# A hybrid block kernel on one core: dependent DVE, ACT and POOL instructions divided into steps of their own

## The chip, the cores and the metric

The kernel runs on one core of one Trainium2 chip. A core has five engines with an in-order queue each: PE (matrix products), DVE (vector work), ACT (activations), POOL (general work) and SP (which here issues DMAs). They meet through semaphores only. The metric is device time in microseconds (us) of one launch; lower is better.

## What is computed

Sixteen sequences of 512 tokens and 256 channels, float32, go through four residual layers:

```python
x = x + mamba(layernorm(x))        # h = exp(dt*A)*h + inp, y = <h, C> + Dp*u, 16 states, a scan over 512 tokens
x = x + ffn(layernorm(x))          # all operands of the three products rounded to FP4 in blocks of 16
x = x + linear_attention(layernorm(x))   # 16 heads of 16, features elu(.)+1, running sums over the tokens
x = x + ffn(layernorm(x))          # the same weights as above

def fp4_quant_dequant(x):          # per block of 16
    scale = max(max(abs(xb)) / 6.0, 1e-12)
    return grid(abs(xb / scale)) * sign(xb) * scale
dt = softplus(dt_low @ w_dt + b_dt) * 0.099 + 0.001
y  = (q @ kv) / (q @ ksum + 1e-6)  # per head, in linear_attention
```

## The kernel before

**Parts.** A batch (one sequence) is worked in parts. `P` is the front of the Mamba layer: load, layernorm, the products x_in, B and dt, and the softplus of dt. `M` has 32 halves of state (16 states by 2 halves of the channels); for each, ACT makes the decay (an Exp and a Square, `decay`), DVE scans over 512 tokens (`scan`, line 1187) and multiplies by C (`read_state`, L1197), and PE sums pairs of states into the bank `acc_y` (`sum_states`, L864, part `G`). `S` and `Y` finish y. `R1` takes the four tiles of 128 tokens through the first FFN (f1) and then linear attention; `R2` takes them through the second FFN (f2), whose layernorm statistics R1 has already taken.

**The FFN in instructions.** Layernorm on DVE (`stats`: a bn_stats, L1139, and a bn_aggr, L1142) with the power on POOL and the normalisation on ACT; block scales on DVE (a maximum L1082, a scaling L1084, a reciprocal L1086, of which each reads the one before); the product with the reciprocal on POOL (L527); the absolute value on ACT; the rounding on DVE (`round_mag`, L1055 and L1057, through the buffer `rounding`); the product with the scale on POOL; turns on PE copied out by ACT (`copy_out`, L667); gate and up products on PE (L896, L899), tanh on ACT (L703), gating on DVE (L1237, L1241, L1245, L1248); the same scales and rounding for the 704 hidden values; the down product (L916) and the residual on DVE (`residual`, L1215).

**Attention.** PE makes q, k and v; ACT makes exp(qk/2) (L724) and squares it (L727, into `a_exp`), copies v (L729, into `vv`); DVE makes the features `fqk` of it (L1264); ACT spreads q over even and odd heads (L734, `q_par`); scores, masked scores (POOL), numerator (PE L974, L981), the sum of k by v (`kv_new`, L1289, and `kv`, L1291), its turn (L996), the division (L1269, L1271, L1273), the turn of y (`yT`) and the projection.

**What sets the order.** The steps of all parts are interleaved by a table written by hand, `TIMES`: for each engine the beat at which a step of a part stands, counted from the part's own first beat (`PARTS_AT`; a batch is 32 beats, one for each half of state). `order_of` sorts all steps of an engine by beat, then batch, then tile. So the scan of half m stands at its beat, and a step of R1 or R2 goes between two scans as a whole, with all its instructions. `Banks` hands out the five rotating PSUM banks in PE's order; `wait_filled` and `wait_drained` are waits on them.

**Waits inside a step.** Where an instruction reads what the one before it on the same engine has written, the engine waits in between on a semaphore that the first one raises. `Chain` counts such steps (`step` and `after`). Some steps also end with a wait on their own last instruction: `round_mag` (on its signal), `residual` and both halves of the gating (on the bank drained), `dt0` and `dt1`, and the sum of kv. An example is L1053 to L1058:

```python
def round_mag(chain, val, mag, signal, b, t):
    chain.step(nc.vector.scalar_tensor_tensor(val[1], mag, ROUNDER, val[0], ALU.max, ALU.subtract))
    chain.after(dve)
    nc.vector.scalar_tensor_tensor(val[0], mag, ROUNDER, val[1], ALU.max, ALU.subtract).then_inc(signal, 1)
    dve.wait_ge(signal, upto(b, TILES, t))
```

The softplus of dt is a step of two parts on ACT (`exp0` and `log0`: Abs, Relu, Exp, three Squares; Ln, Exp, three Squares) and one on DVE (`dt0`: L1160, L1163, L1170), and again for the second half of the channels.

## Time and profile before

| what | value |
|---|---|
| median of 3 runs | 3002.25 us |
| lowest, highest | 3001.89, 3004.42 us |
| span of the profiled execution | 2998.5 us |
| PE busy | 2452.0 us (82%) |
| DVE busy | 2362.8 us (79%) |
| ACT busy | 1899.2 us (63%) |
| POOL busy | 961.6 us (32%) |

The median is 3.75 us over the span of the profiled execution; that much lies around it. A line of the profile names the engine, the line of the code, the operation and the tiles (out<-in, buffer numbers left out); in a timeline it begins with the start and the duration in us, and ends, where the engine had been idle before, with the idle time and what released it, in brackets. xN are N instructions in a row taken together.

### The profile page before, as it was taken

Reading aid. Unit: us, or ns where it says so; the run is one execution under the profiler, and the core shown is the slowest. Engines: PE = TensorE matmul, PEld = TensorE weight load, DVE = VectorE, ACT = ScalarE, POOL = GpSimd, SP = SyncE. Lnnn points to the kernel's source line nnn. Section 1 sums busy time; section 2 is a strip of 40 time slices with the busy share of each in tenths; the row PEclk is TensorE's granted clock in tenths of the full one; section 3 lists DMA queues with packets and bytes.
Section 4 is the critical chain, followed back from the end, with each engine's and each line's share of the span. In section 5 each row is a group of like instructions: output and inputs, shape, how many; then the busy total and the mean of one; then the engine's idle time right before and its main releaser. Section 6 shows DMA issues by size and latency. Waiting matters only on the chain.

```text
span 2998.5 us, 40701 instructions
## 1 busy us (share of the span) xinstructions
PE 2452.0 (82%) x12908; PEld 1394.9 (47%) x12908; DVE 2362.8 (79%) x4136; ACT 1899.2 (63%) x3677; POOL 961.6 (32%) x1632
## 2 busy tenths in 40 slices
PE   3559798888979888797978879798887979879796
PEld 1125354453535445353554535455353545536464
DVE  7776877969788796978879697887969788787744
ACT  4757567685766758576575757658575675846342
POOL 3022332333333233333323233233323323333432
PEclk7669899999999999999999999999999999989898
DMA  3431212112121221212112121211212121121000
GB/s 74 112 88 43 74 46 74 48 50 69 40 78 46 64 55 52 69 41 78 46 46 73 41 77 36 79 46 45 81 39 75 38 81 46 54 58 33 4 5 9
DMA packets 104434, 165.97 MB, mean 55 GB/s; under 512 B 15442, under 2 KB 34078, under 8 KB 104222
## 3 DMA queue, kind: packets, MB, share of 16 engines
q1 hardware_dynamic: 104222, 163.37, 19.8%
q8 instruction: 106, 1.74, 0.2%
q14 instruction: 106, 0.87, 0.1%
HBM read 146.55 MB, written 16.78 MB: 54 GB/s over the span
## 4 chain that ended last, share of the span: by engine, by line
PE 40%; DVE 35%; ACT 17%; issue 5%; POOL 2%; DMA 0%; SPq 0%; DVEq 0%; ACTq 0%; POOLq 0%
PE bank L916 10%; PE bank L899 10%; DVE scan_bufs L1187 7%; DVE scan_bufs L1197 4%; PE acc_y L864 4%; PE bank L956 3%; DVE f_h_max L1082 2%; DVE rounding L1055 2%; ACT p_xT L615 2%; ACT masked_scores L667 2%; PE bank L896 2%; PE bank L937 2%; DVE f_h L1057 2%; PE bank L909 1%; ACT scan_bufs L605 1%
## 5 line engine op out<-in xcount | busy, mean ns | idle before, releaser
L1187 DVE TENSOR_TENSOR_SCAN scan_bufs<-scan_bufs,inp_bank 128x512 f32<-128x512 f32 x512 | 617.2, 1205 | 23.4 <-ACT scan_bufs L607 12.0
L899 PE MATMUL bank<-w_gu,f_xqT 128*128 128x512 f32 x1024 | 496.0, 629 | 52.0 <-ACT f_xqT L667 23.6
L916 PE MATMUL bank<-w_dn,f_hqT 128*128 128x256 f32 (+1 forms) x1536 | 425.6, 423 | 36.3 <-ACT yT L667 33.6
L864 PE MATMUL acc_y<-scan_bufs,sel_y 128*32 128x512 f32 x1024 | 301.5, 673 | 126.9 <-DVE scan_bufs L1197 126.7
L916 PEld LDWEIGHTS bank<-w_dn,f_hqT 128*128 128x128 f32 (+1 forms) x1536 | 296.7, 207 | 155.4 <-issue 78.4
L605 ACT ACTIVATE scan_bufs<-scan_bufs,a_rows 128x512 f32<-128x512 f32 x512 | 365.4, 714 | 4.5 <-DMA scan_bufs<-dt_copy 3.8
L1197 DVE TENSOR_TENSOR scan_bufs<-scan_bufs,c_bank 128x512 f32<-128x512 f32 x512 | 343.5, 671 | 11.8 <-issue 0.2
L899 PEld LDWEIGHTS bank<-w_gu,f_xqT 128*128 128x128 f32 x1024 | 197.4, 201 | 310.1 <-issue 264.0
L607 ACT ACTIVATE scan_bufs<-scan_bufs 128x512 f32<-128x512 f32 x512 | 322.6, 630 | 16.2
L527 POOL TENSOR_TENSOR f_h<-f_h,f_h_inv 128x704 f32<-128x704 f32 x128 | 177.9, 1390 | 368.2 <-DVE f_h_inv L1086 368.2
L527 POOL TENSOR_TENSOR f_h<-f_h,f_h_scale 128x704 f32<-128x704 f32 x128 | 178.1, 1391 | 278.5 <-DVE f_h L1057 278.5
L545 POOL TENSOR_SCALAR_AFFINE_SELECT masked_scores<-masked_scores 128x512 f32<-128x512 f32 x256 | 156.4, 635 | 313.3 <-ACT masked_scores L667 313.2
L703 ACT ACTIVATE f_tanh<-bank 128x512 f32<-128x512 f32 (+1 forms) x256 | 117.3, 458 | 174.1 <-PE bank L899 159.9
L1215 DVE TENSOR_TENSOR x<-bank,x 128x256 f32<-128x256 f32 x192 | 79.9, 416 | 170.2 <-PE bank L916 161.0
L896 PE MATMUL bank<-w_gu,f_xqT 128*128 128x384 f32 x512 | 200.4, 515 | 0.2 <-DVE f_h L1237 0.2
L667 ACT ACTIVATE masked_scores<-bank 128x512 f32<-128x512 f32 x256 | 138.1, 592 | 71.1 <-PE bank L956 70.9
L956 PE MATMUL bank<-q_par,fqk 32*128 32x128 f32 x2048 | 149.0, 283 | 23.7 <-ACT f_hqT L667 8.8
L956 PEld LDWEIGHTS bank<-q_par,fqk 32*128 32x128 f32 x2048 | 125.6, 187 | 87.9 <-issue 58.8
L527 POOL TENSOR_TENSOR f_x<-f_x,f_x_scale 128x256 f32<-128x256 f32 x128 | 80.1, 626 | 259.5 <-DVE f_x L1057 259.5
L864 PEld LDWEIGHTS acc_y<-scan_bufs,sel_y 128*32 128x32 f32 x1024 | 38.5, 112 | 267.7 <-DVE scan_bufs L1197 188.5
L691 ACT ACTIVATE f_h_abs<-f_h 128x704 bf16<-128x704 f32 x128 | 101.2, 790 | 96.8 <-POOL f_h L527 96.8
L672 ACT ACTIVATE f_x<-x,f_below,f_rstd 128x256 f32<-128x256 f32 x128 | 75.8, 592 | 136.2 <-POOL f_below L520 136.2
(194 smaller groups left out, 4610.9 us busy)
## 6 DMA issues: line engine op xcount, KB each, us to landing
scan_bufs<-dt_copy SPq DMA_DIRECT2D x512, 256.0 KB, 3.7
xp<-L_attn_a_x SPq DMA_DIRECT2D x16, 512.0 KB, 4.1
dt_copy<-dt SPq DMA_DIRECT2D x32, 256.0 KB, 2.0
out<-x SPq DMA_DIRECT2D x64, 128.0 KB, 1.7
w_attn<-L_attn_b_W_attn SPq DMA_DIRECT2D x1, 768.0 KB
scan_bufs<-L_ffn_w_gate SPq DMA_DIRECT2D x1, 704.0 KB
scan_bufs<-L_ffn_w_up SPq DMA_DIRECT2D x1, 704.0 KB
masked_scores<-L_ffn_w_down SPq DMA_DIRECT2D x1, 704.0 KB
```

The lines of the kernel that those rows point to most:

```text
L527: pool.tensor_tensor(d, s, spread(scale, width), ALU.mult).then_inc(signal, 1)
L545: pool.affine_select(out=sm[r][:, 4 * g:4 * g + 4, :], in_=sm[r][:, 4 * g:4 * g + 4, :], compare_op=ALU.is_ge, fill=0.0, base=0, pattern=[ ...
L605: nc.scalar.activation(half, half, ACT.Exp, scale=a_rows[:, c, at:at + 1]).then_inc(root_ready, 1)
L607: nc.scalar.activation(half, half, ACT.Square).then_inc(bar_ready, 1)
L667: nc.scalar.activation(dst, src[:, 0:width], ACT.Copy).then_inc(done, 1)
L864: last = nc.tensor.matmul(acc_y[32 * j:32 * j + 32, :], sel_y[:, q, :], bar[slot][:, h, :], start=(q == 0), stop=(q == 3), tile_position=( ...
L896: last = nc.tensor.matmul(to[:, 0:2 * (hi - lo)], f.xqT[:, k, :], w_gu[:, k, :, lo:hi], start=(k == 0), stop=(k == DH - 1))
L899: last = nc.tensor.matmul(to[:, :], f.xqT[:, k, :], w_gu[:, k, g, lo:hi], start=(k == 0), stop=(k == DH - 1))
L916: last = nc.tensor.matmul(to[:, 0:D], f.hqT[0:n, k, :], w_dn[0:n, k, :], start=(k == 0), stop=(k == FK - 1))
L956: last = nc.tensor.matmul(to[:, at:at + P], fqk[r][rows, 1, grp, :], q_par[r][rows, odd, grp, :], start=True, stop=True)
L1187: nc.vector.tensor_tensor_scan(half, half, inp[:, :], 0.0, ALU.mult, ALU.add)\
L1197: nc.vector.tensor_tensor(half, half, c_rep[:, :], ALU.mult).then_inc(read_out, 1)
```

## The change

The steps of two or more dependent instructions are divided: each instruction (or each group without a dependence inside) becomes a step with an entry in `TIMES` and a semaphore of its own. The new steps stand 0.02 to 0.03 beats behind each other, from the beat of the undivided step on. `order_of` sorts by beat and then by batch and tile, so steps of other parts that stand within those hundredths, or at the very beat, go between. The waits at the end of steps go, since whoever reads waits for the new semaphores; so do the semaphore instruction `x4_ready` behind each R2 residual and 16 small copies behind the first kv sums. Buffers change with it: `fqk` is written and squared in place of `a_exp`, `x2` goes (R1 writes `x3`), each FFN has `x_lean` and `h_lean` in place of `rounding`, and the softplus has its buffers once for each half of the channels. ACT and PE get further waits that protect single buffers; the wait for a stored tile (`x4_stored`) moves from the projection's residual to that of the down product.

PE, POOL and SP issue the same instructions in the same order. DVE issues 16 instructions fewer (the copies), ACT as many as before; waits for an instruction that stands directly ahead on the same engine are far fewer on DVE and some fewer on ACT.

The diff, cut to the table, the helpers and the places that the prediction speaks of:

```diff
 TIMES, "act":
-        ("P", "exp0"): 21.8, ("P", "log0"): 22.6, ("P", "exp1"): 24.9, ("P", "log1"): 25.2, ("M", "decay"): -1.2,
-        ("R1", "a_qkv"): 15.0, ("R1", "a_q"): 15.1,
+        ("M", "decay"): -1.2, ("M", "square"): -1.15,
+        ("R1", "a_root"): 15, ("R1", "a_qkv"): 15.05, ("R1", "a_v"): 15.1, ("R1", "a_q"): 15.1,
+        ("P", "abs0"): 21.8, ("P", "exp0"): 21.82, ("P", "sq00"): 21.84, ...
 TIMES, "dve":
-        ("P", "dt0"): 23.1, ("P", "dt1"): 26.05,
-        ("R1", "round_h"): 9.2, ("R1", "a_proj"): 21.1, ("R2", "norm"): 0.8, ...
+        ("P", "soft0"): 23.1, ("P", "sum0"): 23.2, ("P", "dt0"): 23.3, ("P", "soft1"): 26.05, ("P", "sum1"): 26.15, ("P", "dt1"): 26.25,
+        ("R1", "lean_h"): 9.2, ("R1", "round_h"): 9.23, ("R1", "a_proj"): 21.1, ("R1", "stats2"): 21.13, ("R1", "aggr2"): 21.16,
+        ("R2", "max_x"): 0.8, ("R2", "scale_x"): 0.83, ("R2", "norm"): 0.86, ("R2", "lean_h"): 9.4, ("R2", "round_h"): 9.43, ...
...
-            def round_mag(chain, val, mag, signal, b, t):
-
-                chain.step(nc.vector.scalar_tensor_tensor(val[1], mag, ROUNDER, val[0], ALU.max, ALU.subtract))
-                chain.after(dve)
-                nc.vector.scalar_tensor_tensor(val[0], mag, ROUNDER, val[1], ALU.max, ALU.subtract).then_inc(signal, 1)
-                dve.wait_ge(signal, upto(b, TILES, t))
+            def lean(mag, val, out, signal):
+
+                nc.vector.scalar_tensor_tensor(out, mag, ROUNDER, val, ALU.max, ALU.subtract).then_inc(signal, 1)
+
+            def rounded(mag, leaned, val, ready, signal, b, t):
+
+                dve.wait_ge(ready, upto(b, TILES, t))
+                nc.vector.scalar_tensor_tensor(val, mag, ROUNDER, leaned, ALU.max, ALU.subtract).then_inc(signal, 1)
...
+            def block_max(val, width, mx, signal):
+
+                nc.vector.tensor_reduce(mx, blocks(val, width)[0], AX.X, ALU.max, apply_absolute_value=True)\
+                    .then_inc(signal, 1)
+
+            def block_scale(mx, scale, least, ready, signal, b, t):
+
+                dve.wait_ge(ready, upto(b, TILES, t))
+                nc.vector.tensor_scalar(scale, mx, TIES_DOWN / 6.0, least, ALU.mult, ALU.max).then_inc(signal, 1)
+
+            def block_inv(scale, inv, ready, signal, b, t):
+
+                dve.wait_ge(ready, upto(b, TILES, t))
+                nc.vector.reciprocal(inv, scale).then_inc(signal, 1)
...
-            def stats(norm, b, t, x):
-
-                ch.step(nc.vector.bn_stats(norm.st[t][:, :], x))
-                ch.after(dve)
+            def stats(norm, t, x):
+
+                nc.vector.bn_stats(norm.st[t][:, :], x).then_inc(norm.st_ready, 1)
+
+            def aggr(norm, b, t):
+
+                dve.wait_ge(norm.st_ready, upto(b, TILES, t))
                 dve.sem_inc(aggr_allowed, 1)
                 nc.vector.bn_aggr(norm.mv[t][:, :], norm.st[t][:, :]).then_inc(norm.mv_ready, 1)
...
                 src, done = wait_filled(dve, f.part, b, t, use)
                 nc.vector.tensor_tensor(out, src[:, 0:D], x, ALU.add).then_inc(done, 1)
-                wait_drained(dve, f.part, b, t, use)
...
                     dve.wait_ge(a_exp_ready, upto(b, TILES, t))
                     j = uses.bank_of("R1", b, t, "qk")
-                    nc.vector.scalar_tensor_tensor(fqk[r][:, :, :, :].rearrange("p a g n -> p (a g n)"), a_exp[:, :],
-                                                   1.0, banks[j][:, :], ALU.min, ALU.max).then_inc(drained[j], 1)
+                    nc.vector.scalar_tensor_tensor(flat(fqk[r]), flat(fqk[r]), 1.0, banks[j][:, :], ALU.min, ALU.max)\
+                        .then_inc(drained[j], 1)
...
                 act.wait_ge(dt_spread[slot][h], 16 * (nth + 1))
                 (c, at), half = rows_of(m), bar[slot][:, h, :]
                 nc.scalar.activation(half, half, ACT.Exp, scale=a_rows[:, c, at:at + 1]).then_inc(root_ready, 1)
+
+            def square(b, m):
+
+                n, h = divmod(m, DH)
+                half = bar[slot_of(b, n)[0]][:, h, :]
                 act.wait_ge(root_ready, upto(b, HALVES, m))
                 nc.scalar.activation(half, half, ACT.Square).then_inc(bar_ready, 1)
```

Three places where the order itself changes, all on DVE and once or more in each batch. The first is where the second half of dt (`dt1`, beat 26.05) meets the residual and statistics of R1's projection and the features of the next tile (`fqk`). Before:

```order
L1160 SCALAR_TENSOR_TENSOR p_xT<-p_xT 128x512
L1163 SCALAR_TENSOR_TENSOR sp_log<-p_xT,sp_log 128x512
L1170 SCALAR_TENSOR_TENSOR dt<-sp_log,sp_pos 128x512
L1215 TENSOR_TENSOR x_0<-bank,x 128x256
L1139 BN_STATS f_st<-x_0 128x6
L1142 BN_AGGR f_mv<-f_st 128x2
L1264 SCALAR_TENSOR_TENSOR fqk<-a_exp,bank 128x512
L1289 TENSOR_TENSOR kv_new<-bank,headmask 128x272
L1291 TENSOR_TENSOR kv<-kv,kv_new 128x16x17
L1187 SCALAR_TENSOR_TENSOR scan_bufs<-scan_bufs,inp_bank 128x512
```

and after:

```order
L1216 SCALAR_TENSOR_TENSOR p_xn<-p_xn 128x512
L1273 TENSOR_TENSOR x_0<-bank,x_0 128x256
L1335 SCALAR_TENSOR_TENSOR fqk<-fqk,bank 128x512
L1189 BN_STATS f_st<-x_0 128x6
L1222 SCALAR_TENSOR_TENSOR dt<-p_xn,dt 128x512
L1195 BN_AGGR f_mv<-f_st 128x2
L1229 SCALAR_TENSOR_TENSOR dt<-dt,sp_pos 128x512
L1359 TENSOR_TENSOR kv_new<-bank,headmask 128x272
L1364 TENSOR_TENSOR kv<-kv,kv_new 128x16x17
L1245 SCALAR_TENSOR_TENSOR scan_bufs<-scan_bufs,inp_bank 128x512
```

The three dt instructions (L1160, L1163, L1170; after, L1216, L1222, L1229) no longer stand together: the residual, fqk and the statistics go between, and the last two of them stand behind fqk.

The second place is at beat 23.1, where the rounding of h in R2 meets the same steps of another tile and the first half of dt. Before:

```order
L1055 SCALAR_TENSOR_TENSOR rounding<-f_h_abs,f_h 128x704
L1057 SCALAR_TENSOR_TENSOR f_h<-f_h_abs,rounding 128x704
L1215 TENSOR_TENSOR x_0<-bank,x 128x256
L1139 BN_STATS f_st<-x_0 128x6
L1142 BN_AGGR f_mv<-f_st 128x2
L1264 SCALAR_TENSOR_TENSOR fqk<-a_exp,bank 128x512
L1160 SCALAR_TENSOR_TENSOR p_xT<-p_xT 128x512
L1163 SCALAR_TENSOR_TENSOR sp_log<-p_xT,sp_log 128x512
L1170 SCALAR_TENSOR_TENSOR dt<-sp_log,sp_pos 128x512
L1289 TENSOR_TENSOR kv_new<-bank,headmask 128x272
```

and after:

```order
L1097 SCALAR_TENSOR_TENSOR f_h_lean<-f_h_abs,f_h 128x704
L1273 TENSOR_TENSOR x_0<-bank,x_0 128x256
L1335 SCALAR_TENSOR_TENSOR fqk<-fqk,bank 128x512
L1216 SCALAR_TENSOR_TENSOR p_xT<-p_xT 128x512
L1102 SCALAR_TENSOR_TENSOR f_h<-f_h_abs,f_h_lean 128x704
L1189 BN_STATS f_st<-x_0 128x6
L1195 BN_AGGR f_mv<-f_st 128x2
L1222 SCALAR_TENSOR_TENSOR dt<-p_xT,dt 128x512
L1359 TENSOR_TENSOR kv_new<-bank,headmask 128x272
L1229 SCALAR_TENSOR_TENSOR dt<-dt,sp_pos 128x512
```

The second instruction of the rounding (L1057; after, L1102) stood directly behind the first and ahead of the residual; it now stands behind the residual, fqk and the first dt instruction.

The third place is in R2, where the scales of the hidden values of one tile meet those of the next tile's x. Before:

```order
L1084 TENSOR_SCALAR f_h_scale<-f_h_max 128x44
L1086 RECIPROCAL f_h_inv<-f_h_scale 128x44
L1082 TENSOR_REDUCE f_x_max<-f_x 128x16
L1084 TENSOR_SCALAR f_x_scale<-f_x_max 128x16
L1086 RECIPROCAL f_x_inv<-f_x_scale 128x16
L1197 TENSOR_TENSOR scan_bufs<-scan_bufs,c_bank 128x512
```

and after:

```order
L1135 TENSOR_SCALAR f_h_scale<-f_h_max 128x44
L1129 TENSOR_REDUCE f_x_max<-f_x 128x16
L1140 RECIPROCAL f_h_inv<-f_h_scale 128x44
L1135 TENSOR_SCALAR f_x_scale<-f_x_max 128x16
L1140 RECIPROCAL f_x_inv<-f_x_scale 128x16
L1255 TENSOR_TENSOR scan_bufs<-scan_bufs,c_bank 128x512
```

The maximum of x goes ahead of the reciprocal of h's scale, and the scaling of x's maximum follows that reciprocal directly.

On ACT the Square of a decay now stands behind the Abs, Relu or Exp of dt's first half where they meet (once in a batch), and the copy of v (`a_v`, line 766 after) stands behind the two q copies (771) in place of ahead of them, in each of the 64 tiles.

## Rows read from the trace of the kernel before

**Rows 1.** The page: busy time of each engine; engines on the chain.

```profile
PE 2452.0 (82%) x12908; PEld 1394.9 (47%) x12908; DVE 2362.8 (79%) x4136; ACT 1899.2 (63%) x3677; POOL 961.6 (32%) x1632
...
PE 40%; DVE 35%; ACT 17%; issue 5%; POOL 2%; DMA 0%; SPq 0%; DVEq 0%; ACTq 0%; POOLq 0%
```

**Rows 2.** Timeline of DVE: the first scans of batches 2 and 15 (start, duration).

```profile
328.13 1.22 DVE L1187 TENSOR_TENSOR_SCAN scan_bufs<-scan_bufs,inp_bank 128x512 f32<-128x512 f32 x1
...
2622.28 1.22 DVE L1187 TENSOR_TENSOR_SCAN scan_bufs<-scan_bufs,inp_bank 128x512 f32<-128x512 f32 x1 [0.22 <-DVE x L1215]
```

**Rows 3.** Stretches: PE, PEld, DVE, ACT, POOL busy (instructions), PE clock, DMA, GB/s.

```profile
328.10:2622.30 2294.20, 1950.47 (x10452) 1114.51 (x10451) 1872.73 (x3304) 1532.90 (x2967) 764.03 (x1303) 0.95 0.21 58
...
1390.00:1423.00 33.00, 19.80 (x62) 7.63 (x59) 30.90 (x60) 16.56 (x31) 10.07 (x22) 0.84 0.41 116
```

**Rows 4.** Timeline of DVE: a dependent pair in the rounding of h.

```profile
1271.55 0.88 DVE L1055 SCALAR_TENSOR_TENSOR rounding<-f_h_abs,f_h 128x704 f32<-128x704 bf16 x1
...
1272.46 0.89 DVE L1057 SCALAR_TENSOR_TENSOR f_h<-f_h_abs,rounding 128x704 f32<-128x704 bf16 x1
```

**Rows 5.** R2's scale of x, nine of them: nanoseconds min/median/max.

```profile
L1084 DVE TENSOR_SCALAR f_x_scale<-f_x_max x9: 174/593/1187, 1324.3 to 1501.2; 128x16 f32<-128x16 f32 x9
```

**Rows 6.** Timeline: R2's scales of x, and PE's sum behind the read.

```profile
1414.64 1.38 POOL L527 TENSOR_TENSOR f_h<-f_h,f_h_inv 128x704 f32<-128x704 f32 x1 [2.92 <-DVE f_h_inv L1086]
...
1414.88 1.18 DVE L1084 TENSOR_SCALAR f_x_scale<-f_x_max 128x16 f32<-128x16 f32 x1
...
1416.26 0.63 DVE L1197 TENSOR_TENSOR scan_bufs<-scan_bufs,c_bank 128x512 f32<-128x512 f32 x1
...
1416.94 0.62 PE L864 MATMUL acc_y<-scan_bufs,sel_y 128*32 128x512 f32 x2 [1.65 <-DVE scan_bufs L1197]
```

**Rows 7.** Timeline: an aggregate ahead of a scan, and PE's sum behind the read.

```profile
1404.12 0.18 DVE L1142 BATCH_NORM_AGGREGATE f_mv<-f_st 128x2 f32<-128x6 f32 x1 [0.50 <-DVE f_st L1139]
...
1406.95 0.62 PE L864 MATMUL acc_y<-scan_bufs,sel_y 128*32 128x512 f32 x2 [0.56 <-DVE scan_bufs L1197]
```

**Rows 8.** Timeline: the place beat 26.1 (dt1, residual, stats, fqk).

```profile
1358.63 0.69 DVE L1160 SCALAR_TENSOR_TENSOR p_xT<-p_xT 128x512 f32<-128x512 f32 x1 [6.57 <-ACT p_xT L615]
...
1360.19 0.67 ACT L724 ACTIVATE a_exp<-bank,minus_half 128x512 f32<-128x512 f32 x1
...
1360.81 0.42 DVE L1215 TENSOR_TENSOR x<-bank,x 128x256 f32<-128x256 f32 x1
...
1360.89 0.63 ACT L727 ACTIVATE a_exp<-a_exp 128x512 f32<-128x512 f32 x1
...
1361.26 0.43 DVE L1139 BATCH_NORM_STATS2 f_st<-x 128x6 f32<-128x256 f32 x1
...
1361.28 3.70 PE L899 MATMUL bank<-w_gu,f_xqT 128*128 128x512 f32 x8 [1.49 <-DVE x L1215]
...
1361.43 0.36 ACT L729 ACTIVATE vv<-bank 128x256 f32<-128x256 f32 x1
...
1361.84 0.18 DVE L1142 BATCH_NORM_AGGREGATE f_mv<-f_st 128x2 f32<-128x6 f32 x1
1361.93 0.65 DVE L1264 SCALAR_TENSOR_TENSOR fqk<-a_exp,bank 128x512 f32<-128x512 f32 x1
...
1364.70 0.69 DVE L1197 TENSOR_TENSOR scan_bufs<-scan_bufs,c_bank 128x512 f32<-128x512 f32 x1
```

**Rows 9.** Timeline: the place beat 23.1 (rounding of h, fqk, the turn of h).

```profile
1338.67 0.69 DVE L1264 SCALAR_TENSOR_TENSOR fqk<-a_exp,bank 128x512 f32<-128x512 f32 x1 [0.68 <-ACT a_exp L727]
...
1339.11 1.38 POOL L527 TENSOR_TENSOR f_h<-f_h,f_h_scale 128x704 f32<-128x704 f32 x1
...
1343.12 0.63 PE L909 MATMUL bank<-ident,f_h 128*128 128x128 f32 x4 [0.46 <-DVE kv_new L1289]
```

**Rows 10.** Timeline of PE: the down product after a wait.

```profile
1327.83 5.36 PE L916 MATMUL bank<-w_dn,f_hqT 128*128 128x256 f32 x12 [2.42 <-ACT yT L667]
```

**Rows 11.** That down product as a stretch (columns of rows 3).

```profile
1328.00:1333.20 5.20, 5.20 (x14) 3.47 (x16) 0.00 (x0) 5.15 (x8) 1.81 (x3) 0.55 0.02 5
```

345 lines of the change are left out of this document (193 added, 152 removed), and 45 rows, old and new, of the table TIMES.

## The prediction, as put on record before the run

> **What bounds the kernel now.** I read the page's busy line and the engines on its chain first. PE is busy 2452.0 us of 2998.5, DVE 2362.8, ACT 1899.2, POOL 961.6, and the chain that ended last lies 40% on PE, 35% on DVE, 17% on ACT [rows 1]. No engine bounds the kernel alone: PE and DVE take turns. Second, the timeline's scans: the first scan of batch 2 starts at 328.13 and that of batch 15 at 2622.28 [rows 2], so the 13 batches between take 176.5 us each. The batches before and the last one (2622 to the end, 376 us) hold the same steps spread thinner. Third, that stretch as a window: PE busy 1950.47 of 2294.20 [rows 3], so PE is idle 343.7 us, or 26.4 us a batch. That is all a DVE or ACT edit can win, and only where DVE or ACT is what PE waits for. Fourth I walked through one batch, from 1252 to 1429 us, and listed each PE wait with its releaser. From 1252 to 1290 PE never waits. Then come small waits, and the densest stretch is 1390 to 1423: DVE busy 30.90 of 33 us and PE only 19.80 [rows 3], PE waiting for the read of a state three times, among them 0.56 us at 1406.95 [rows 7] and 1.65 us at 1416.94 [rows 6], and last for the turned x of P, which ACT copies out.
>
> **What a dependence costs.** In the rounding the second instruction starts at 1272.46, and the first ended at 1271.55 + 0.88 = 1272.43: 0.03 us later [rows 4]. With no dependence the next instruction starts ahead of the end: the features start at 1361.93, and the aggregate ended at 1361.84 + 0.18 = 1362.02, so 0.09 earlier [rows 8]. The difference is 0.12 us. With a semaphore instruction in between (stats to aggregate) it is 1361.84 - (1361.26 + 0.43) = +0.15, so 0.24 against no wait [rows 8]. ACT is alike: the Square starts 1360.89 - (1360.19 + 0.67) = +0.03, and the copy of v behind it 1361.43 - (1360.89 + 0.63) = -0.09 [rows 8], again 0.12. Counted in the two programs, DVE loses 994 such adjacencies, 198 of them with the semaphore instruction, and ACT 90. One batch loses 64 plain and 13 others on DVE: 64 x 0.12 + 13 x 0.1 = about 9 us of DVE's time. DVE is 33 us idle in each batch (1872.73 of 2294.20 busy [rows 3]), so most of this only makes DVE idle longer.
>
> The Trainium skill, VectorE: DVE Perf Modes, section "The DRAIN you can't avoid", speaks against the change: it says of back-to-back copies that "the semaphore costs nothing extra here". By that rule the term above would be zero, and what the change would do is then rival D. The rows here show 0.12 us, so this trace disagrees.
>
> **The change, place by place, in this one batch.** Each term is how much earlier (-) or later (+) PE gets on.
>
> *Scale of x in R2, twice a batch.* Today POOL's product with h's reciprocal starts at 1414.64, and DVE's scaling of x's maximum, which follows, takes 1.18 us (to 1416.06) instead of 0.174 [rows 5, 6]: it ends with POOL's instruction (1416.02). After the change it stands directly behind the reciprocal, so it starts before POOL does, and then takes 0.17: -1.0. The Trainium skill, SBUF — State Buffer, "Who interferes with whom", says the port pair shared by DVE and GpSimd is an exclusive lock that whoever starts first holds to the end of its instruction. By that rule POOL would be the one to wait 0.1 us, with nothing else changed. The second of the two lies before a wait of PE for other work and gives nothing.
>
> *Aggregate behind a scan.* The aggregate of f1 waits 0.50 us for its stats at 1404.12 [rows 7]; now a scan goes between, so that 0.50 goes, and 0.24 - 0.12 or so of the semaphore instruction with it: -0.65. With one rounding pair and its end wait (2 x 0.12) and less one further scan-side wait, the read that PE waits for at 1406.95 comes 0.93 earlier. PE waits only 0.56 there, so it gains that and then fills up behind ACT. The next read, at 1416.26 [rows 6], comes 0.93 + 1.0 earlier less 0.1 for a tanh that is then late: -1.83, of which PE can use all, since its waits between are 1.5 (for ACT's turned x) and 1.65. Two more dependences up to 1423 make **-2.06** for this stretch. What was cut here is late next on ACT (the tanh and the turned x).
>
> *Beat 23.1, once a batch.* The second rounding instruction now stands behind the features, which wait for a_exp's Square until 1338.64 (the features wait 0.68 there [rows 9]), and behind one dt instruction. It ends at about 1340.8 instead of 1336.7. Behind it POOL's product with the scale (1.38 us, at 1339.11 [rows 9]) runs 1342.6 to 1344.0, and PE's turn of h, which starts at 1343.12 after a wait of 0.46 for another bank [rows 9], starts 0.9 later. Other PE work stands behind it with waits of its own (the down product waits for nothing else), and 0.37 of the 0.9 is left: **+0.37**.
>
> *Beat 26.1, once a batch.* The dt instructions stand at 1358.63, ahead of the residual at 1360.81, for which PE waits 1.49 us [rows 8]. Now the residual goes behind the first of them, 1.4 earlier, and PE's wait is gone. But the features then wait for a_exp's Square, which ends at 1361.52 [rows 8], with the statistics and two dt instructions of 0.69 now behind them in DVE's queue, and behind these the sum of kv, the scan and the read. The read today at 1364.70 [rows 8] comes about 1.1 later, and PE, whose next sum follows it half a microsecond behind, goes on **+0.67** later than now. This is the head-of-line wait that the division brings: before, the 2.07 us of dt filled the time up to the Square.
>
> *Order of ACT, four tiles a batch.* The copy of v (0.36 us [rows 8]) now stands behind the q copies, and its bank and the numerator wait for it. In three tiles that is covered by 1.8 us or more of slack in the v bank. In one the turned numerator is 0.27 late: **+0.27**. It can cost at most the 0.36 in each of four tiles (+1.4), and at least nothing.
>
> *Rest.* Three ACT dependences (3 x 0.12) in front of PE's wait for the turned y at 1325: -0.36, say -0.40 with the DVE share. One DVE dependence at 1290 that is soon bound by a_exp: -0.15. One in the division: -0.12. Together **-0.67**. The x4_stored wait moves 11 beats or more behind the store it needs, the 16 copies are once a batch at 0.1 us, the Squares behind Abs and Relu delay a decay 2.5 us that runs several halves ahead of the scan. I cost these at nothing; if the decay's cover were gone, the scan would lose up to 2.5 once a batch.
>
> Sum: -2.06 + 0.37 + 0.67 + 0.27 - 0.67 = -1.42 us a batch. Thirteen batches give -18.5, and the first two and the last, with the same steps but more idle time, about -4 more: -22 on the span, so 2998.5 - 22 = 2976.5. With 3.75 us around the span, as now (3002.25 - 2998.5), that is **2980**. The profiled execution and the median go together, so no more is to be shifted.
>
> **The rivals.**
> B. *All chain dependences count.* If every DVE stretch between PE's waits shortens (I count 4.1 us of dependences on them a batch, and the 1.0 of the scale) and the two places lose nothing, it is -5.1 x 13 = -66, with the ends -70: 2932. For it: DVE is on 35% of the chain [rows 1]. Against: ACT and PE stand close behind in most waits, and the two places are in the listing.
> C. *Slower: the features' wait pulls PE's clock down.* PE would stand idle around 1364 about 0.65 and again 1.9 us, where it now works on without a break (8 products in 3.70 [rows 8]). After such a wait of 2.42 us, at 1325, twelve products took 5.36 us [rows 10] at a granted clock of 0.55 [rows 11], near the lower level of 1.2 GHz: 5.36 x 0.45 = 2.4 us lost. Once or twice a batch that is +2.4 to +4.8, less 1.4: +1.0 to +3.4, and over 13 batches and the ends 3017 to 3048; 3030 in the middle. It decides from the point at which these two waits bring the clock to the lower level at 1364, which the trace of before does not show.
> D. *No difference.* The 0.12 us do not carry to PE, or semaphore waits further apart cost the same. Then the late terms +1.31 stand against the scale (-1.0) and the aggregate's 0.50: -0.2 a batch, 3000. The change is made as it says (the order of DVE shows it), so that is no rival.
>
> **How the numbers follow.** Chances: A (2980, own range 2964 to 2994, from half and twice the late terms, 0.7 to 2.6 us x 13) 0.57; B 0.11; C 0.17; D 0.15. A measurement here tells about 0.2%, 6 us, from no change. A and B are faster: 0.68. D is the same: 0.15. C is slower: 0.17. The range takes in A and D whole and the lower half of C, and stops short of B: 2952 to 3030, with 0.11 + 0.08 left out.
>
> **What would show each step right or wrong.** In the profile of after: R2's scale of x at 0.17 us in all instances; the aggregate without its 0.50; the 13 batches at about 175.1 us instead of 176.5; DVE's busy time the same but for the 1.0 us pieces, and its idle time some 7 us a batch up; features waiting over 1 us for a_exp at beat 26.1, with the next read about 1 us later within its batch; PE's wait for the residual (1.49) gone; PE's busy time near 2450, so the clock as now. Busy time of PE up by over 20 us at the same work would be C. An unchanged start-to-start distance of instructions that are no longer dependent would be D. The prediction is wrong above all if the two places of late fqk cost more than the 1.04 I gave them, since I walked one batch of thirteen, or if the stretch from 1390 to 1423 is bound by ACT sooner than I think.

## The result, and the profile after

The changed kernel is slower: 3038.99 us median (3024.57 to 3045.09, 4 runs) against 3002.07 us (3001.18 to 3004.42), a ratio of 1.0118 with a 95% interval of 1.0092 to 1.0143. I had forecast 2980. The profiled execution took 3045.09 us and its span is 3043.4 us, at the upper end of its runs, so its trace shows some 6 us more than the median.

The page of the changed kernel, busy time of each engine and the engines on the chain (as rows 1):

```profile
PE 2529.1 (83%) x12908; PEld 1426.1 (47%) x12908; DVE 2247.3 (74%) x4120; ACT 1896.1 (62%) x3677; POOL 985.6 (32%) x1632
...
PE 51%; DVE 20%; ACT 19%; issue 6%; POOL 3%; DMA 0%; SPq 0%; DVEq 0%; ACTq 0%; POOLq 0%
```

DVE's busy time fell by 115 us, and DVE's share of the chain from 35% to 20%. But PE, with the same 12908 matmuls, is busy 77 us longer (2452.0 in [rows 1]). That is the first thing to see, since my prediction named it as the sign of rival C. The granted clock goes with it: over the 13 batches it is 0.91 in the first window row below, where it was 0.95 [rows 3].

Timeline of the changed kernel's DVE: the first scans of batches 2 and 15 (as rows 2), then stretches (columns of rows 3): the 13 batches between, and 33 us that begin 3.3 us behind a first scan, as 1390 to 1423 do:

```profile
329.58 1.22 DVE L1245 TENSOR_TENSOR_SCAN scan_bufs<-scan_bufs,inp_bank 128x512 f32<-128x512 f32 x1
...
2674.64 1.21 DVE L1245 TENSOR_TENSOR_SCAN scan_bufs<-scan_bufs,inp_bank 128x512 f32<-128x512 f32 x1
```

```profile
329.60:2674.60 2345.00, 2027.28 (x10451) 1145.01 (x10450) 1770.30 (x3290) 1530.19 (x2966) 785.82 (x1301) 0.91 0.20 56
1234.20:1267.20 33.00, 22.07 (x64) 8.65 (x65) 31.67 (x66) 19.43 (x38) 11.74 (x24) 0.81 0.43 116
```

A batch takes 180.4 us (2345.06 / 13) in place of 176.5 [rows 2]. PE's idle time in it went from 26.4 us to (2345.00 - 2027.28) / 13 = 24.4: 2.0 less, so its waits as a whole did become shorter. PE's busy time went from 1950.47 / 13 = 150.0 [rows 3] to 155.9: 5.9 more. The sum is +3.9 us a batch, 51 us in 13. The last batch is 7.4 us shorter than before (3043.4 - 2674.6 = 368.8 against 376.2), and the 13 batches begin 1.5 us later.

**Where the clock falls.** To lay the same batch of both kernels side by side I count from its first scan, at 1210.05 before and 1230.90 after. The next batch begins at 1386.64 and 1411.83, so this one takes 176.6 us before and 180.9 after.

```profile
1210.05 1.22 DVE L1187 TENSOR_TENSOR_SCAN scan_bufs<-scan_bufs,inp_bank 128x512 f32<-128x512 f32 x1 [0.22 <-DVE x L1215]
```

```profile
1230.90 1.21 DVE L1245 TENSOR_TENSOR_SCAN scan_bufs<-scan_bufs,inp_bank 128x512 f32<-128x512 f32 x1
```

Timeline of PE before, behind the place beat 23.1 (turn of h, last dt product, state sum, down product, turn of y), and that stretch's window (columns of rows 3, granted clock third from the end):

```profile
1343.12 0.85 PE L909 MATMUL bank<-ident,f_h 128*128 128x128 f32 x6 [0.46 <-DVE kv_new L1289]
1343.89 1.12 PE L834 MATMUL bank<-dt_low,w_dt 64*128 64x512 f32 x2
1345.48 1.05 PE L864 MATMUL acc_y<-scan_bufs,sel_y 128*32 128x512 f32 x4 [0.46 <-DVE scan_bufs L1197]
1346.46 3.05 PE L916 MATMUL bank<-w_dn,f_hqT 128*128 128x256 f32 x12
```

```profile
1343.40:1350.20 6.80, 6.34 (x32) 3.43 (x31) 5.77 (x12) 6.25 (x13) 1.84 (x3) 1.00 0.41 118
```

The same of the changed kernel, with DVE and POOL ahead of it:

```profile
1356.87 0.69 DVE L1335 SCALAR_TENSOR_TENSOR fqk<-fqk,bank 128x512 f32<-128x512 f32 x1 [2.72 <-ACT fqk L763]
...
1358.07 0.88 DVE L1102 SCALAR_TENSOR_TENSOR f_h<-f_h_abs,f_h_lean 128x704 f32<-128x704 bf16 x1
...
1359.44 0.18 DVE L1195 BATCH_NORM_AGGREGATE f_mv<-f_st 128x2 f32<-128x6 f32 x1
...
1359.70 0.55 POOL L534 TENSOR_TENSOR f_var<-f_mv,eps_col 128x1 f32<-128x1 f32 x1 [4.95 <-DVE f_mv L1195]
...
1361.15 1.59 POOL L551 TENSOR_TENSOR f_h<-f_h,f_h_scale 128x704 f32<-128x704 f32 x1
...
1362.80 0.88 PE L949 MATMUL bank<-ident,f_h 128*128 128x128 f32 x6 [1.69 <-POOL f_h L551]
1363.61 1.57 PE L874 MATMUL bank<-dt_low,w_dt 64*128 64x512 f32 x2
1365.10 1.92 PE L904 MATMUL acc_y<-scan_bufs,sel_y 128*32 128x512 f32 x4
1366.95 5.02 PE L956 MATMUL bank<-w_dn,f_hqT 128*128 128x256 f32 x12
```

```profile
1364.20:1371.00 6.80, 6.80 (x16) 3.38 (x14) 2.58 (x5) 4.96 (x10) 0.62 (x1) 0.50 0.15 40
```

PE waits 1.69 us for POOL's product in place of 0.46 for a bank, and 1.4 us behind the end of that wait the clock is at 0.50, the 1.2 GHz level: the four state sums take 1.92 instead of 1.05 and the twelve down products 5.02 instead of 3.05. The features are reached 2.65 us earlier within the batch (1356.87 - 1230.90 = 125.97 against 1338.67 - 1210.05 = 128.62 [rows 9]); the turn of h only 1.17 earlier; the end of the down products is 1.6 later ((1371.97 - 1230.90) - (1349.51 - 1210.05)).

The second place follows 28 us on. Before, PE went from the score products to the turn of y without a wait; now it waits 2.13 us for the divided y, and the clock falls again. Before, then after with its window:

```profile
1366.86 1.16 PE L956 MATMUL bank<-q_par,fqk 32*128 32x128 f32 x16
1367.95 0.44 PE L1001 MATMUL bank<-ident,y_tok 128*128 128x128 f32 x2
```

```profile
1391.32 0.55 PE L1043 MATMUL bank<-ident,y_tok 128*128 128x128 f32 x2 [2.13 <-DVE y_tok L1349]
1391.80 2.08 PE L995 MATMUL bank<-q_par,fqk 32*128 32x128 f32 x16
```

```profile
1391.50:1398.30 6.80, 6.80 (x28) 3.47 (x26) 3.33 (x5) 3.00 (x8) 3.31 (x3) 0.50 0.22 70
```

The sixteen score products take 2.08 us there; at full clock they take 1.16. In the 13 batches of the kernel before, the clock never falls at either place; in those of the changed kernel it falls at both places in every one.

### The profile page after: what moved, and what is told of

The parts are those of the page before. It is cut to its first block, busy times and chain, and to the rows that moved or that the text cites. A ratio compares the mean times of both kernels' runs of the same rounds, so it can differ in the third digit from the quotient of the medians.

```text
span 3043.4 us, 40582 instructions
## 1 busy us (share of the span) xinstructions
PE 2529.1 (83%) x12908; PEld 1426.1 (47%) x12908; DVE 2247.3 (74%) x4120; ACT 1896.1 (62%) x3677; POOL 985.6 (32%) x1632
## 4 chain that ended last, share of the span: by engine, by line
PE 51%; DVE 20%; ACT 19%; issue 6%; POOL 3%; DMA 0%; SPq 0%; DVEq 0%; ACTq 0%; POOLq 0%
PE bank L956 12%; PE bank L939 11%; PE acc_y L904 5%; PE bank L936 4%; PE bank L995 3%; DVE scan_bufs L1245 3%; PE bank L863 2%; PE bank L977 2%; PE bank L949 2%; DVE scan_bufs L1255 2%; PE bank L869 2%; ACT scan_bufs L629 2%; DVE fqk L1335 1%; ACT masked_scores L697 1%; ACT fqk L759 1%
## 5 line engine op out<-in xcount | busy, mean ns | idle before, releaser
L956 PE MATMUL bank<-w_dn,f_hqT 128*128 128x256 f32 (+1 forms) x1536 | 443.5, 437 | 40.5 <-ACT yT L697 37.1
L904 PE MATMUL acc_y<-scan_bufs,sel_y 128*32 128x512 f32 x1024 | 322.6, 716 | 92.0 <-DVE scan_bufs L1255 91.6
L956 PEld LDWEIGHTS bank<-w_dn,f_hqT 128*128 128x128 f32 (+1 forms) x1536 | 309.5, 215 | 175.7 <-issue 90.6
L936 PE MATMUL bank<-w_gu,f_xqT 128*128 128x384 f32 x512 | 214.1, 545 | 0.1
L995 PE MATMUL bank<-q_par,fqk 32*128 32x128 f32 x2048 | 160.4, 298 | 18.8 <-ACT f_hqT L697 10.2
L995 PEld LDWEIGHTS bank<-q_par,fqk 32*128 32x128 f32 x2048 | 135.7, 200 | 83.9 <-issue 83.9
L534 POOL TENSOR_TENSOR f_var<-f_mv,eps_col 128x1 f32<-128x1 f32 x128 | 35.2, 275 | 405.4 <-DVE f_mv L1195 405.4
L949 PE MATMUL bank<-ident,f_h 128*128 128x128 f32 (+1 forms) x768 | 111.7, 283 | 48.5 <-POOL f_h L551 48.3
```

What stands on the lines that cost most here:

```text
L904: last = nc.tensor.matmul(acc_y[32 * j:32 * j + 32, :], sel_y[:, q, :], bar[slot][:, h, :], start=(q == 0), stop=(q == 3), tile_position=( ...
L936: last = nc.tensor.matmul(to[:, 0:2 * (hi - lo)], f.xqT[:, k, :], w_gu[:, k, :, lo:hi], start=(k == 0), stop=(k == DH - 1))
L949: last = nc.tensor.transpose(to[0:n, k * P:(k + 1) * P], f.h[r][:, lo:lo + n], ident[:, :])
L956: last = nc.tensor.matmul(to[:, 0:D], f.hqT[0:n, k, :], w_dn[0:n, k, :], start=(k == 0), stop=(k == FK - 1))
L995: last = nc.tensor.matmul(to[:, at:at + P], fqk[r][rows, 1, grp, :], q_par[r][rows, odd, grp, :], start=True, stop=True)
```

## The experiments

Twelve kernels. Medians are in us; the ratio is to the kernel before, with its 95% interval. The text below counts batches from 0, so the 13 batches are 2 to 14, and the one laid side by side above is batch 7.

| run | what it is | median | ratio |
|---|---|---|---|
| e1_round | changed, beat 23.1's rounding undone | 3005.31 | 1.0013 (1.0004 to 1.0022) |
| e2_dt1 | changed, second half of dt in one piece | 3019.07 | 1.0054 (1.0037 to 1.0071) |
| e3_both | e1 and e2 together | 2960.65 | 0.9867 (0.9853 to 0.9882) |
| e4_v | changed, copy of v first | 3016.88 | 1.0052 (1.0037 to 1.0067) |
| e5_best | e3, statistics and copy of v first | 2955.94 | 0.9852 (0.9837 to 0.9867) |
| e6_dose | e3 + 0.89 us ahead of the rounding | 2970.43 | 0.9898 (0.9884 to 0.9913) |
| e7_scale | e3, R2's scale of x behind POOL's start | 2993.72 | 0.9982 (0.9972 to 0.9991) |
| e8_flat | changed, all in the order of before | 2994.04 | 0.9975 (0.9966 to 0.9985) |
| e9_dose_s | e3 + 0.41 us ahead of the statistics | 2997.12 | 0.9985 (0.9976 to 0.9994) |
| e10_dose_l | e3 + 0.82 us there | 2999.49 | 0.9995 (0.9985 to 1.0005) |
| e11_flat_scale | e8, one swap of scale | 2987.76 | 0.9951 (0.9937 to 0.9966) |
| e12_opt | e5, beat 26.1 in order of readiness | 2926.72 | 0.9747 (0.9732 to 0.9761) |

**The two places.** The theory after the result: each late wait of PE at the two places costs its own length and then a fall of the clock. The rivals are in what was written down for each run. The three dt instructions stand 0.1 beats apart in the table, more than the 0.02 to 0.03 given above for the new steps, so more can come between them.

```diff
# e1_round
-("R2", "lean_h"): 9.4, ("R2", "round_h"): 9.43
+("R2", "lean_h"): 9.4, ("R2", "round_h"): 9.4
# e2_dt1
-("P", "sum1"): 26.15, ("P", "dt1"): 26.25
+("P", "sum1"): 26.05, ("P", "dt1"): 26.05
# e3_both: both
```

e1_round. 

> The changed kernel with one entry of the table moved: R2's second rounding instruction stands directly behind the first again (round_h at 9.4 instead of 9.43), everything else as changed. Theory 1 (the wait at the features, then the clock): PE waits 1.69 us for POOL's product with h's scale at +130 us of each batch, the clock falls to 1.2 GHz for 6.83 us at +133, and this costs about 0.9 + 3.4 us a batch. Then here the slow stretch at +133 is gone and the time is 3039 - 13 x 4 = about 2987 (2980 to 3000). Theory 2 (the clock falls whatever stands there, since PE is shifted as a whole against where it was): the slow stretch at +133 stays, time 3030 to 3040. Theory 3 (only the second place, beat 26.1, matters): 3030 to 3039.

e2_dt1. 

> The changed kernel with the three instructions of dt's second half in one piece again (sum1 and dt1 at 26.05), and those of the first half left divided. Theory 1: PE's wait for y_tok (2.13 us at +158) comes from the features' wait with dt's instructions and the sum of kv behind them; without it the slow stretch at +160 is gone and the time is 3039 - 13 x 3 = about 3000 (2990 to 3015). The slow stretch at +133 stays. Rival: the wait at +158 is handed down from the place 28 us before (PE and DVE late out of step by then), and the second half of dt has no part in it: 3033 to 3042, slow stretch at +160 unchanged.

e3_both. 

> The changed kernel with both of these places undone. Theory 1 (both places, their costs add): neither slow stretch, the batches at about 173.5 us (the gain of 2 to 3 us a batch up to +130 is kept), 2955 to 2975. If the gain is given back in waits elsewhere: 2990 to 3003. If something else lowers the clock: 3010 or more.

Undoing the first place gives 34 us and the second 20, each short of what I expected of it by 15 to 20 and outside its range, and both together 78. Each edit takes away the wait it was made for. In e1_round PE waits 0.89 us at the first place in all 13 batches and the clock doesn't fall there; the wait of 2.13 and its fall stay at the second. In e2_dt1 the wait for y is gone, so it was not handed down from the first place. Both together give more than the sum: with one place left, its slow stretch stays, in some batches other slow stretches are longer too, and batches of 175 us stand beside batches of 180. With both undone, the batch is at 174.1 us throughout. Timeline of e3_both at the place beat 23.1, and its window:

```profile
1328.80 0.87 PE L949 MATMUL bank<-ident,f_h 128*128 128x128 f32 x6 [0.89 <-POOL f_h L551]
1329.60 1.12 PE L874 MATMUL bank<-dt_low,w_dt 64*128 64x512 f32 x2
1330.65 1.05 PE L904 MATMUL acc_y<-scan_bufs,sel_y 128*32 128x512 f32 x4
1331.64 3.05 PE L956 MATMUL bank<-w_dn,f_hqT 128*128 128x256 f32 x12
```

```profile
1331.00:1334.30 3.30, 3.30 (x15) 2.11 (x12) 1.78 (x4) 3.24 (x6) 0.62 (x1) 1.00 0.07 18
```

PE's wait is 0.89 and the clock stays at 1.00; the matmuls take what they took before. Three entries of the table are thus the difference between 1.2% slower and 1.3% faster.

But e2_dt1 also shows that the length of the wait doesn't decide alone. PE waits 1.69 us at the first place in all 13 batches, as in the changed kernel, and in two of them (8 and 10) no fall follows. Batch 8 there, and its window:

```profile
1535.35 0.87 PE L949 MATMUL bank<-ident,f_h 128*128 128x128 f32 x6 [1.69 <-POOL f_h L551]
1536.15 1.12 PE L874 MATMUL bank<-dt_low,w_dt 64*128 64x512 f32 x2
1537.20 1.05 PE L904 MATMUL acc_y<-scan_bufs,sel_y 128*32 128x512 f32 x4
1538.18 3.05 PE L956 MATMUL bank<-w_dn,f_hqT 128*128 128x256 f32 x12
```

```profile
1536.70:1543.50 6.80, 6.80 (x42) 4.07 (x40) 5.08 (x8) 6.05 (x13) 0.63 (x2) 1.00 0.11 39
```

**The copy of v.**

```diff
# e4_v
-("R1", "a_v"): 15.1
+("R1", "a_v"): 15.06
```

> The changed kernel with the copy of v ahead of the two q copies on ACT again, in all tiles; DVE as changed. Theory 1 prices this at 0.27 us a batch and no clock: 3031 to 3039. Rival: the late copy of v makes the numerator, its turn and y late in each tile and is what PE waits for at +158: the slow stretch at +160 goes, 2995 to 3010.

It gave 22 us, between my two cases. I had priced it at 0.27 us a batch, 4 us in all. Most batches of its profile take 177 us and two of the middle ones 183 and 185. The rival fails too, since neither long wait became shorter. Timeline of PE in batch 7 of e4_v, and two windows laid as those of the changed kernel above:

```profile
1359.34 0.88 PE L949 MATMUL bank<-ident,f_h 128*128 128x128 f32 x6 [1.89 <-POOL f_h L551]
...
1386.18 0.41 PE L1043 MATMUL bank<-ident,y_tok 128*128 128x128 f32 x2 [2.21 <-DVE y_tok L1349]
```

```profile
1360.90:1367.70 6.80, 6.80 (x29) 3.42 (x30) 3.25 (x6) 5.18 (x9) 0.62 (x1) 0.75 0.09 27
1388.20:1395.00 6.80, 6.74 (x53) 3.41 (x51) 4.66 (x11) 2.44 (x6) 2.83 (x5) 0.75 0.20 61
```

The waits are 1.89 and 2.21 us, longer than 1.69 and 2.13, and the clock still falls behind them, but it is back sooner: 0.75 over each window, where the changed kernel has 0.50. What does become shorter is PE's wait for the turned numerator ahead of the first place: 0.43 us in batch 7 of the changed kernel, 0.21 here. That this is why the slow stretches are shorter is not shown. On e3_both the same move together with the statistics (e5) is worth 5 us.

**The dose.** Here the question is whether a longer wait of PE brings the clock down when nothing else in the order is changed. The edits put maxima into a spare tile, once a batch.

```diff
# e6_dose, on e3_both, ahead of the second rounding instruction (round_h of f2, tile 2)
+nc.vector.tensor_reduce(spare[:, :], blocks(f.h_abs[:, :], F)[0], AX.X, ALU.max)
# e9_dose_s (one) and e10_dose_l (two), on e3_both, ahead of stats2 of tile 0
+for i in range(1 or 2):
+    nc.vector.tensor_reduce(spare[:, i, :], blocks(x3[par][:, t, :], D)[0], AX.X, ALU.max)
```

e6_dose. 

> e3_both plus one maximum over 128x704 (0.89 us, into a spare tile) ahead of the second rounding instruction of R2's third tile, once a batch, at the place of beat 23.1: no other order, no features in it. Theory: PE's wait for POOL's product with h's scale grows from 0.89 (as in e3_both) to 1.7 or 1.8, the clock falls at +133 in all or most batches, and the 0.89 us of work costs 3 to 5 us a batch: 3000 to 3030. Rival (the clock has nothing to do with this wait; the time is only the delay itself): 0 to 0.9 us a batch, 2961 to 2973, slow time a batch as in e3_both.

It cost 10 us, inside the rival's bounds, but it doesn't decide the question: PE's wait for POOL's product stayed at 0.88 us, since the added 0.89 us lay ahead of the features, which waited 1.59 us instead of 1.79. It showed me that what holds PE's turn of h is not the rounding. POOL takes the power of the projection's variance (L534 to L544) ahead of its product with h's scale, and the aggregate that it needs stands behind the features. The second rounding instruction was late only as one more thing in front of that aggregate. One batch of e6_dose bears on the question by accident: in batch 13 PE waited 1.20 us, the clock fell behind it, and the batch took 176.0 us where its neighbours took 174.0 and 174.8.

e9_dose_s. 

> e6_dose did not reach PE: its 0.89 us were hidden in the features' wait, since what PE's turn of h waits for at +130 is not the rounding but the statistics behind the features (POOL takes the power of their variance ahead of the product with h's scale). So here, on e3_both, one maximum over 128x256 (0.41 us, into a spare tile) stands right ahead of the statistics of R1's first tile, behind the features, once a batch. Theory: PE's wait for POOL's product at +130 grows from 0.89 to about 1.3; whether the clock falls there is open, this is a point of the dose. Without a fall: 0 to 0.4 us a batch, 2961 to 2966. With one: 3 to 4 us a batch, 3000 or more.

e10_dose_l. 

> As e9, with two such maxima (0.82 us). PE's wait at +130 grows from 0.89 to about 1.7, as in the changed kernel. Theory (the clock falls by that wait): a slow stretch at +133 in the batches, and 0.8 us of added DVE work costs 3 to 5 us a batch: 3000 to 3025. Rival (the wait costs only itself): at most 0.8 us a batch, 2961 to 2972, and no slow stretch at +133.

PE in e9_dose_s, then in e10_dose_l, at the turn of h, and the windows behind it:

```profile
1347.71 0.87 PE L950 MATMUL bank<-ident,f_h 128*128 128x128 f32 x6 [1.21 <-POOL f_h L552]
```

```profile
1349.50:1352.80 3.30, 3.30 (x8) 1.36 (x8) 2.19 (x4) 3.24 (x6) 0.62 (x1) 0.50 0.26 61
```

```profile
1343.03 0.87 PE L950 MATMUL bank<-ident,f_h 128*128 128x128 f32 x6 [1.53 <-POOL f_h L552]
```

```profile
1344.90:1348.20 3.30, 3.30 (x9) 1.36 (x9) 2.11 (x4) 3.23 (x6) 0.62 (x1) 0.51 0.13 30
```

With 0.41 us of added DVE work once a batch, PE's wait goes from 0.89 to 1.21, the clock falls behind it in 9 of the 13 batches, and the kernel loses 36 us. Over the 13 batches that is 2.8 us a batch ((2631.27 - 331.96) / 13 = 176.9 against 174.1), far more than the 0.41. So a small delay of PE at this place is enough to lower the clock, and that the delay costs only itself is refuted. Not all of the 36 us lies at this place: two of the batches take 181 us, with longer slow stretches elsewhere, and make some 15 of it.

Doubling the dose raises the wait to 1.53, the clock falls in 10 of 13 batches, and the median is 2 us higher, which is not clear of noise (the two intervals overlap). So from 1.21 us on the length of the wait matters little here. But it is no threshold: at 0.89 no batch falls, at 1.21, 1.53 and 1.69 (e2_dt1) most do and 4, 3 and 2 of 13 do not, with the same wait. What sets those batches apart the runs don't show. For the small dose I had written down 2961 to 2966 without a fall and 3000 or more with one; 2997 lies in neither, near the second. Of the large one I had expected 3000 or more, which it missed by half a microsecond.

**What the division itself brings.**

```diff
# e5_best, on e3_both
-("R1", "stats2"): 21.13, ("R1", "aggr2"): 21.16, ("R1", "a_v"): 15.1
+("R1", "stats2"): 21.1, ("R1", "aggr2"): 21.1, ("R1", "a_v"): 15.06
# e7_scale, on e3_both
-("R2", "max_x"): 0.8
+("R2", "max_x"): 0.83
# e8_flat: every new step at the beat of the step that it was cut from
# e11_flat_scale, on e8_flat
-("R2", "inv_h"): 7.7, ("R2", "max_x"): 0.8
+("R2", "inv_h"): 7.705, ("R2", "max_x"): 0.703
```

e5_best. 

> e3_both with two more places undone: the statistics behind R1's projection ahead of the features again (stats2 and aggr2 at 21.1), and the copy of v ahead of the q copies on ACT. If each of the reorderings behind the features' wait only costs, this is the fastest: 2950 to 2961. If the copy of v mattered in the changed kernel only by the clock (e4_v gave 22 us), and e3_both has no slow stretch left for it to remove: within 5 us of e3_both's 2960.65.

e7_scale. 

> e3_both with R2's maximum of x behind the reciprocal of h's scale again (max_x at 0.83), so that the scaling of x starts behind POOL's product. Theory: it takes up to 1.18 us again instead of 0.17, PE's reads between +20 and +35 us come 1.0 later, and this is worth 1.0 us a batch: 2960.65 + 13 = 2974 (2968 to 2980). Rival (the chain there is ACT's and hides it): 2959 to 2964.

e8_flat. 

> The changed kernel with all steps of a divided chain at the very beat of the first one, on DVE and ACT: the order of every engine is that of the kernel before (but for the 16 small copies), and what remains of the change is the semaphores, the buffers and the waits at the end of steps that went. If the gain lies in those end waits alone (about a fifth of the 994 dependences): 2990 to 2998. If it lies in instructions put between dependent ones: 2998 to 3004. If the further protective waits on ACT and PE cost something: above 3004.

e11_flat_scale. 

> e8_flat (the order of the kernel before) with one swap alone: R2's maximum of the next x ahead of the reciprocal of h's scale, in 45 places (three of four tiles of 15 batches), so that the scaling of x starts before POOL's product. Theory: the scaling takes 0.17 us instead of up to 1.18 and PE gains 0.7 to 1.1 us a batch: 2994 less 9 to 15, 2979 to 2985. If e7_scale's 33 us was this term whole: 2961 to 2970. If the chain hides it in this order: 2990 to 2996.

e5_best fits both of its cases, so it doesn't decide between them. In batch 7 of its profile PE has no wait at the turn of h any more, which agrees with the statistics being what that turn waited for.

e8_flat keeps the order of before and is 7 us faster, inside the first case. That is the net of what it does change: the waits at the end of steps, the copies, the buffers and the further waits on ACT and PE. It doesn't tell these apart. The gain of the good order over e8_flat (e3_both, 33 us more) lies in what stands between dependent instructions. The scale of x is one such piece. The source view of that line, in the changed kernel (nanoseconds min/median/max), and in e7_scale:

```profile
L1135 DVE TENSOR_SCALAR f_x_scale<-f_x_max x11: 109/175/596, 1285.2 to 1523.7; 128x16 f32<-128x16 f32 x11
```

```profile
L1135 DVE TENSOR_SCALAR f_x_scale<-f_x_max x9: 174/593/1191, 1318.8 to 1497.2; 128x16 f32<-128x16 f32 x9
```

Put back behind POOL's start, it takes up to 1.19 us again, and the kernel loses 33 us, two and a half times the 13 that I expected. In batch 7, scan 8 comes 1.1 us later within the batch, as I had priced it, and scan 12 still 0.7. Another 1.2 us is lost at the end of this batch, and the trace shows where: behind PE's wait for the residual the clock falls, though the wait is no longer than the one in e3_both, behind which it stays up. Batch 7 of e7_scale, then of e3_both, each with a window:

```profile
1355.33 5.40 PE L939 MATMUL bank<-w_gu,f_xqT 128*128 128x512 f32 x8 [1.51 <-DVE x L1273]
```

```profile
1356.00:1359.30 3.30, 3.30 (x6) 1.24 (x5) 3.09 (x7) 0.77 (x2) 1.01 (x4) 0.50 0.69 238
```

```profile
1346.35 3.70 PE L939 MATMUL bank<-w_gu,f_xqT 128*128 128x512 f32 x8 [1.51 <-DVE x L1273]
```

```profile
1347.00:1350.30 3.30, 3.05 (x8) 1.02 (x6) 3.09 (x7) 1.93 (x5) 1.01 (x4) 1.00 0.84 255
```

Batches 5, 8 and 10 of e7_scale show the same fall. Put in alone, into the order of before (e11), the same swap gives 6 us and not 9 to 15, and there batches of 174 stand beside batches of 177 us with longer slow stretches. The two don't agree on the price of this piece: its direct part is shown, and what it sets off later differs with the rest of the order.

**A better order.** e3_both and e5_best keep the order of before at the place beat 26.1. There PE waits 1.5 us for the residual, which stands behind three dt instructions and is ready before them.

```diff
# e12_opt, on e5_best
-("R1", "a_qkv"): 15.1, ("P", "soft0"): 23.1, ("P", "soft1"): 26.05, ("P", "sum1"): 26.05, ("P", "dt1"): 26.05
+("R1", "a_qkv"): 15.12, ("P", "soft0"): 23.13, ("P", "soft1"): 26.11, ("P", "sum1"): 26.11, ("P", "dt1"): 26.11
```

> e5_best with the place beat 26.1 put in the order of readiness: residual, statistics, aggregate, the three dt instructions, then the features (dt's second half at 26.11, the features' step at 15.12 and soft0 at 23.13, which keeps all other orders). The residual's source is ready about 1.4 us before DVE takes it, and PE waits 1.5 us for it in e5_best. Theory: PE's wait goes to 0.5 or less without delaying the features, worth 0.5 to 1 us a batch: 2955.9 less 6 to 13, 2943 to 2950. Rival: PE's next wait (the read behind the scan) takes it back: 2953 to 2958.

It is the fastest of all, 2926.72 us, 29 us under e5_best where I had expected 6 to 13. The batches take 171.3 us in the mean (2226.7 / 13). Timeline of e12_opt at this place, DVE and PE:

```profile
1328.92 0.69 DVE L1216 SCALAR_TENSOR_TENSOR p_xn<-p_xn 128x512 f32<-128x512 f32 x1 [3.54 <-ACT p_xn L693]
...
1331.71 0.69 DVE L1335 SCALAR_TENSOR_TENSOR fqk<-fqk,bank 128x512 f32<-128x512 f32 x1 [0.64 <-ACT fqk L763]
...
1332.45 1.13 PE L939 MATMUL bank<-w_gu,f_xqT 128*128 128x512 f32 x2 [0.79 <-DVE fqk L1335]
```

```profile
326.90:2553.60 2226.70, 1930.71 (x10399) 1105.50 (x10450) 1784.11 (x3291) 1524.74 (x2966) 780.99 (x1302) 0.95 0.22 59
```

The residual and its statistics are done before dt's instructions have their data (DVE waits 3.54 us for ACT), dt then fills the time up to the features' Square, and the features wait 0.64 us for it. In the changed kernel they waited 1.76 at this place:

```profile
1383.88 0.69 DVE L1335 SCALAR_TENSOR_TENSOR fqk<-fqk,bank 128x512 f32<-128x512 f32 x1 [1.76 <-ACT fqk L763]
```

The clock is back at 0.95 in the mean. Why the gain is more than twice what I expected I have not taken apart; a part of it may be the clock, since a slow stretch some 34 us into the batch, present in 11 of 13 batches of e5_best, is present in 3 of 13 here.

## Why the prediction was wrong

**The gain was there.** "the 13 batches at about 175.1 us" was summed from -2.06, -0.67 and +1.31. Up to the features at beat 23.1 the changed kernel is 2.65 us ahead within the batch, where my terms up to there (-2.06, -0.15, -0.40, +0.27) make 2.34. At the end of the stretch for which I had summed -2.06, PE starts on the turned x of P at 1265.58, 34.7 us into the batch, where before it was 37.1 (1423.76 - 1386.64): 2.4 earlier. The scale of x takes 0.17 in most instances. e3_both, which is the change less its two bad places, measured 174.1 us a batch; my terms without those two (-2.06 + 0.27 - 0.67 = -2.46) make 174.0. That the sum fits so well is in part luck: the scale of x, 1.0 in it, was worth 33 / 13 = 2.5 us a batch when it was taken out of e3_both, and 6 / 13 = 0.5 when it was put in alone.

**The step that failed is the price of a wait.** The sum for +0.37 at "Beat 23.1" counted the delay of PE and put the fall of the clock behind it at nothing. I had PE's turn of h start 0.9 us later, on top of a wait of 0.46, and called 0.37 of it left. The wait became 1.69. The features waited 2.72 us where they had waited 0.68, since the second rounding instruction, the statistics and the aggregate (0.88, 0.42 and 0.18 us) no longer filled the time up to ACT's Square but stood behind it. The path was off too: I had POOL's product wait for the rounding, but e6_dose and e9_dose_s show that it is held by the power of the variance, whose aggregate comes last. The direct loss is 2.65 - 1.17 = 1.5. And then the clock fell, which cost (1.92 - 1.05) + (5.02 - 3.05) + (1.57 - 1.12) = 3.3 us on the next 18 matmuls, of which I had counted none; less the wait of 0.46 ahead of the state sums, which went, it is 2.8 by the end of the down products (1.17 + 1.6). So this place cost 4.3 us in this batch and not 0.37. The dose runs show that a wait of 1.2 us, less than the 1.3 or so that I had forecast for this place, lowers the clock in most batches.

**Beat 26.1** I had at +0.67. The scan behind it started at 156.06 us of the batch (1386.96 - 1230.90) against 153.40 (1363.45 - 1210.05): 2.7 later, of which 1.6 were lost already, so 1.1 at this place, as I had said of the read. PE's wait for the residual went, as I said, and PE then waited 0.46 for the features. PE's next sum was only 0.3 later in the batch (1387.05 - 1230.90 = 156.15 against 1365.88 - 1210.05 = 155.83). But DVE was 2.7 late, and PE met that at the turn of y: a wait of 2.13 where there had been none. That brought the clock down a second time: 0.9 us on the sixteen score products alone. From 1.6 behind at the end of the down products the batch went to 4.3 behind at its end (180.9 - 176.6), 2.7 for the second place.

**Rival C was the case**, with 0.17 of the chances: a head-of-line wait at the features, PE's waits grown by it, the clock at 1.2 GHz behind them, 3017 to 3048. Its price of a fall (2.4 us, from the down product at half clock [rows 10, 11]) was near the 2.8 of the first place. Its sign came true: PE's busy time rose by 77 us, over the 20 that I had named. Its place was off: I put both waits around 1364, where PE still had work; they were at the turn of h and at y's turn. I had said that "the trace of before does not show" where the point of decision lies. By the lengths of waits alone I could not have found it there: PE had waits of 0.92 and 1.49 us in this batch without a fall and one of 2.42 with one, so a wait of 1.3 would have looked safe, and it was not. A wait at that place had two prices, its own length and that plus about 3 us, and I took the lower without a row that spoke for it.

**Rivals B and D** fell: e8_flat is 7 us under the kernel before, so what the change does without a new order is not nothing. B had no loss at the two places, and e3_both, where that is so, is 41 us under the kernel before and not 70. e12_opt passes B with 75, but by an order at beat 26.1 in which dt's three instructions stand together again. **The copy of v** was mis-sized: 0.27 us a batch forecast, 22 us of the whole in e4_v, where the slow stretches behind both long waits became shorter. **DVE's busy time** I had said to stay the same but for the scales. It fell by 115 us, of which the scales of x are 33 (67.3 us for all 128 of them before, 34.5 after). Most of the rest is that instructions which no longer wait start 0.09 us ahead of the end of the one before and overlap is counted once: an estimate from 994 of them is 89 us. Its idle time in the 13 batches rose by 12 us a batch (44.2 from 32.4), where I had said 7. **The range of A** doesn't follow from its own words: with half and twice the late terms (0.7 and 2.6 us x 13) the sum gives about 2971 to 2997, not 2964 to 2994. The result lies outside both.
